# Window-attention block on one core: attention and projection on four 64x64 quadrants of the array, with a reordered round

## Chip, cores, metric

The kernel runs on one core of one Trainium2 chip. Its time is the device time of one launch in microseconds (us); the figure of a kernel is the median of its runs. Engines are called by the profile's names: PE (TensorE, matmuls), PEld (PE's weight loads), DVE (VectorE), ACT (ScalarE), POOL (GpSimd), SP (SyncE, which issues most DMAs).

## What is computed

The input is 32 images of 64 channels and 16x16 pixels, in fp32. The reference, cut to what matters:

```python
x = x + _conv_bn(x, dw0_w, dw0_s, dw0_b, groups=C)          # 3x3 depthwise
x = x + _ffn(x, f0_w1, ..., f0_b2)                          # 64 -> 128 -> 64
x = x + _windowed_attn(x, wq, wkv, pos, scale_p, dwc_w, dwc_b, proj_w, proj_b)
x = x + _conv_bn(x, dw1_w, dw1_s, dw1_b, groups=C)
x = x + _ffn(x, f1_w1, ..., f1_b2)
# _windowed_attn: windows of 7x7 of the padded 21x21 image, 4 heads of 16
q = (relu(q) + 1e-06) / sc;  k = (relu(k + pos) + 1e-06) / sc
q, k = _focus(q), _focus(k)            # t**3, scaled back to the norm of t
z = 1.0 / (einsum('bic,bc->bi', q, k.sum(axis=1)) + 1e-06)
kv2 = einsum('bjc,bjd->bcd', k, v);  y = einsum('bic,bcd,bi->bid', q, kv2, z)
y = y + depthwise_5x5(v) + dwc_b       # within the window
return y @ proj_w.T + proj_b
```

## The kernel before

The 32 images are worked in NG = 8 groups g of four images. A tile such as `x2[:, g, :]` has 128 partitions (`a` = 0 or 1 picks the partition half, 64 channels each) and 512 columns (`j` = 0 or 1, each image's 256 pixels): four images as 2 x 2. There are 16 stages `m`: m = 0 to 7 are the first depthwise convolution and FFN of group m, m = 8 to 15 the second ones of group m-8. Between them stands the attention of the group. The instruction streams of all engines are written out by hand and are held together by semaphores (`wait_ge`); each engine runs its own stream in order.

The main loop has one **round** for each n = 2 to 8. In round n, PE does in this order: `project_qkv` of group n-1 (L570, L580); `attend` of group n-3 (L645); `turn_fm` of group n-5, a transpose of the 5x5 convolution's result (L691, L695); `key_sum` of group n-2 (L613 to L615); `ffn2` of stage n+1 (L543); `key_value` of group n-2 (L601, L605); `conv` of stage n+2 (L513); `project_out` of group n-5 (L703); `turn_q` of group n-2 (L625, L628); in rounds 4 and 8 the 5x5 window convolution of four groups, `window_conv` (L665, and L671 for the bottom rows); and `ffn1` of stage n+2 (L533). In rounds 2 to 4 there is no `turn_fm` and no `project_out`.

DVE has in a round: `k_raw` (L811), `q_t` (L803), `k_t` (L819), `q_dot` (L856), `cubes` (L827), `residual` (L795), `q_sum` (L861), `add_fm` (L893), `q_scale`, `q_final` (L883, L886), `attended` (L903), `norm2` (L831), `norm6` (L835 to L837), `k_focus` (L850). ACT has: `take_v` (L375, L377), `take_y` (L413), `squares` (L384), `sixth` (L390), `take_kv` (L407), `widened` (L360), `take_qt` (L398), in rounds 4 and 8 `take_fm` (L424), `ratio` (L394), `hidden` (L368). POOL masks the values for `key_value`.

After the last round a written-out tail works off groups 4 to 7 and the stages 11 to 15. The second convolution reads its input through memory: `attended(g)` fills `x3`, a DMA writes it out (`bounce` on SP for g < 5, `write_back` on ACT for g = 5 to 7), and three DMAs of `spread(g)` read it back in a shifted form into `xr`, for which `conv(8+g)` waits.

PSUM has 8 banks of 128 x 512 fp32. Bank 0 holds the convolution, the result of `ffn2` and that of `attend`; banks 1 and 2 (`P_H`) hold the two halves of `ffn1`, and in turn `turn_fm` (1) and `project_out` (2); banks 3 to 7 hold q, k and v of a group, and later `key_value` (3 to 5) and `key_sum` (6, 7).

`attend` multiplies each of the 9 windows of an image with that window's 64x64 matrix. An image of partition half a uses rows and columns of the array at 64a, so the two halves of the array's diagonal work side by side and the other two quadrants stand idle:

```python
src = qt[p, j, :].rearrange("p (h w) -> p h w", w=HW)[:, ry, rx]
dst = ps[p, PX * j:PX * j + PX]
last = eng.matmul(dst, kv[p, slot, :], src, start=True, stop=True)
```

`project_out` is one matmul of 512 columns with a 128x128 weight matrix whose off-diagonal 64x64 blocks are zero. In fp32 each matmul of the program shows as two weight loads and two matmul records in the trace.

## Time and profile before

| | us |
|---|---|
| median of the 3 timed runs | 191.64 |
| lowest, highest | 189.98, 191.72 |
| time of the profiled execution | 189.52 |
| span of the profiled execution | 187.7 |

The span runs from the first to the last instruction of the program on the core; 1.8 us of the profiled execution's own time lie outside it. PE is busy for 93% of the span, DVE for 68%, ACT for 48%, POOL for 19%. A row of the timeline gives the start, the busy time, the engine, the line of the kernel, what is written and read, the number of records, and in brackets how long the engine had been idle before and what released it. The engines' records overlap, so the length of a step is best read as the distance between two starts.

### The profile page before, as it was taken

To read this page: it belongs to the slowest core of one execution; us is meant where nothing else is said; L and a number is where in the kernel's file an instruction comes from. 1 tells how busy PE (TensorE), PEld (TensorE's weight loads), DVE (VectorE), ACT (ScalarE), POOL (GpSimd) and SP (SyncE) were. 2 spreads that over 40 slices of the span, in tenths; PEclk is the share of its full clock that TensorE was granted. 3 is DMA by queue.
4 is the path that set the end of the run, shared out by engine and by line. 5 is a ranking of instruction groups with operands and counts; after the bars stand their busy time and mean duration, and the time that the engine had idled before them with its cause. 6 is when DMAs were issued, how large, how long until landed. Compare 5 with 4: busy or idle time off the path is not lost.

```text
span 187.7 us, 4600 instructions
## 1 busy us (share of the span) xinstructions
PE 173.9 (93%) x1874; PEld 94.7 (50%) x1874; DVE 127.5 (68%) x245; ACT 90.8 (48%) x148; POOL 36.0 (19%) x79
## 2 busy tenths in 40 slices
PE   7989868999999999899989989998998999999982
PEld 6423223537537549673674475375286652642310
DVE  3653897399899592459859886895971396148851
ACT  1474362584494595348265455734843205512340
POOL 3000180062071080006202600900620000000000
PEclk9999999999999999999999999999999999999998
DMA  5999860609600000000260170153126025994931
GB/s 144 233 260 235 159 161 2 161 3 200 191 2 3 0 0 3 3 0 0 71 170 3 59 175 3 56 155 82 59 71 166 0 80 182 268 223 128 236 105 64
DMA packets 16150, 19.33 MB, mean 103 GB/s; under 512 B 3216, under 2 KB 11664, under 8 KB 16128
## 3 DMA queue, kind: packets, MB, share of 16 engines
q1 hardware_dynamic: 15552, 17.86, 39.2%
q10 hardware_dynamic: 576, 1.17, 1.9%
q8 instruction: 15, 0.25, 0.6%
q14 instruction: 7, 0.06, 0.1%
HBM read 14.70 MB, written 4.33 MB: 101 GB/s over the span
## 4 chain that ended last, share of the span: by engine, by line
PE 66%; DVE 22%; ACT 5%; issue 4%; POOL 0%; DVEq 0%; ACTq 0%; POOLq 0%
PE ps L513 13%; PE ps L543 8%; PE ps L533 5%; PE ps L703 5%; PE ps L613 4%; PE ps L601 4%; PE ps L505 4%; PE ps L665 4%; PE ps L645 4%; DVE nrm L835 3%; DVE nrm L831 3%; PE ps L709 3%; PE ps L605 3%; DVE kraw L811 2%; DVE t L827 2%
## 5 line engine op out<-in xcount | busy, mean ns | idle before, releaser
L344 POOL TENSOR_SCALAR vmt<-vbot,cst 128x64 f32<-128x64 f32 x48 | 17.0, 377 | 100.6 <-PE ps L605 80.1
L513 PE MATMUL ps<-xr,dwst 96*32 96x480 f32 (+1 forms) x288 | 32.1, 579 | 0.0
L368 ACT ACTIVATE hid<-ps,fst 128x512 f32<-128x512 f32 x32 | 20.1, 680 | 18.2 <-PE ps L533 18.2
L407 ACT ACTIVATE kv<-ps,cst 128x288 f32<-128x288 f32 x32 | 19.8, 785 | 8.6 <-PE ps L605 8.6
L533 PE MATMUL ps<-x,w1t 64*128 64x512 f32 x64 | 18.1, 638 | 4.8 <-ACT x L360 3.1
L543 PE MATMUL ps<-hid,w2t 128*64 128x512 f32 x64 | 18.4, 618 | 1.6 <-ACT hid L368 1.6
L645 PEld LDWEIGHTS ps<-qt,kv 64*64 64x64 f32 x576 | 17.4, 135 | 2.7 <-issue 2.6
L513 PEld LDWEIGHTS ps<-xr,dwst 96*32 96x32 f32 x288 | 8.3, 109 | 20.3 <-issue 19.5
L645 PE MATMUL ps<-qt,kv 64*64 64x14 f32 (+2 forms) x576 | 18.1, 210 | 0.0
L390 ACT ACTIVATE s<-t 128x1152 f32<-128x1152 f32 x8 | 9.3, 1163 | 17.5 <-DVE t L827 15.0
L334 POOL TENSOR_SCALAR vmb<-vband,cst 128x512 f32<-128x512 f32 x24 | 17.7, 750 | 0.0
L856 DVE TENSOR_TENSOR q<-ps,t 128x576 f32<-128x576 f32 x8 | 6.1, 758 | 15.1 <-PE ps L615 15.1
L570 PEld LDWEIGHTS ps<-wqkv,x 64*128 64x128 f32 x128 | 11.1, 186 | 5.3 <-issue 5.0
L850 DVE TENSOR_TENSOR kf<-t,foc 112x512 f32<-112x512 f32 (+1 forms) x16 | 6.6, 454 | 8.9 <-ACT foc L394 8.9
L570 PE MATMUL ps<-wqkv,x 64*128 64x192 f32 x128 | 12.5, 327 | 0.0
L375 ACT ACTIVATE vband<-ps 128x512 f32<-128x512 f32 x8 | 4.8, 597 | 15.1 <-DVE tqk L803 15.1
L601 PE MATMUL ps<-vmb,kf 128*64 128x192 f32 x128 | 11.8, 327 | 0.0
L601 PEld LDWEIGHTS ps<-vmb,kf 128*64 128x64 f32 x128 | 9.1, 137 | 5.0 <-issue 4.0
L893 DVE TENSOR_TENSOR y<-y,ps 128x512 f32<-128x512 f32 x8 | 5.4, 680 | 8.9 <-ACT y L413 5.5
L533 PEld LDWEIGHTS ps<-x,w1t 64*128 64x128 f32 x64 | 5.0, 184 | 12.8 <-ACT x L360 5.4
L827 DVE TENSOR_TENSOR t<-sq,tqk 128x1152 f32<-128x1152 f32 x8 | 10.8, 1356 | 0.3 <-ACT sq L384 0.3
L613 PE MATMUL ps<-kf,cst 128*128 128x512 f32 x16 | 8.7, 624 | 2.2 <-ACT vbot L377 2.2
(113 smaller groups left out, 259.9 us busy)
## 6 DMA issues: line engine op xcount, KB each, us to landing
xr<-x_out SPq DMA_DIRECT2D x16, 264.0 KB, 4.6
xr<-in_x SPq DMA_DIRECT2D x16, 240.0 KB, 5.4
xr<-x_out SPq DMA_DIRECT2D x8, 272.0 KB, 3.6
xr<-in_x SPq DMA_DIRECT2D x8, 256.0 KB, 4.4
out<-y SPq DMA_DIRECT2D x8, 256.0 KB, 3.3
x_out<-x SPq DMA_DIRECT2D x5, 272.0 KB, 2.1
x_out<-x ACTq DMA_DIRECT2D x3, 272.0 KB, 3.2
tband<-in_matrix SPq DMA_DIRECT2D x1, 784.0 KB, 6.1
```

The source lines that it names most:

```text
L334: last = eng.tensor_scalar(vmb[:, w, :, :], vband[:, g, :, :], cc("win_band")[:, w:w + 1], 0.0, ALU.mult, ALU.add)
L344: last = eng.tensor_scalar(vmt[:, w, :], vbot[:, g, :], cc("win_bot")[:, w:w + 1], 0.0, ALU.mult, ALU.add)
L368: eng.activation(hid[:, m % 2, a, :], bank(P_H + a), ACT.Relu, bias=ff(f"f{s}b1")).then_inc(h_ready, 1)
L407: last = eng.activation(kv[:, :, :].rearrange("p (k s) c -> p k (s c)", k=3)[:, :, h:384:NH], src[:, :, h:384:NH], ACT.Copy, scale=cc("hea ...
L513: last = eng.matmul(dst[:, :, max(-dx, 0):HW - max(dx, 0)], dwst[:, s, tile % 2, dx + 1, :], taps_of(m, tile, dx), start=(dx == 0), stop=( ...
L533: eng.matmul(bank(P_H + a), w1t[p, s, :], x1[p, m % 2, :], start=True, stop=True).then_inc(h_ps, 1)
L543: last = eng.matmul(ffn_bank(m)[64 * a:64 * a + 64], w2t[:, s, :], hid[:, m % 2, a, :], start=True, stop=True)
L570: eng.matmul(qkv()[:, 4 * a + t, 0:3 * C], x2[p, g, at:at + 128], wqkv[p, :, :].rearrange("p s c -> p (s c)"), start=True, stop=True)
L601: eng.matmul(ps[64 * a:64 * a + 64, o:o + 192], kf[:, 4 * a + t, :], vmb[:, :, 2 * t + a, :], start=True, stop=True)
L613: eng.matmul(ps[:, o:o + 512], cc("mask_band"), kf[:, 0:8, :].rearrange("p s c -> p (s c)"), start=True, stop=True)
L645: last = eng.matmul(dst, kv[p, slot, :], src, start=True, stop=True)
L827: eng.tensor_tensor(t3[:, g % 2, :, :], sq[:, :, :], tqk[:, g % 2, :, :], ALU.mult).then_inc(t3_ready, 1)
```

## The change

1. **Attention on four quadrants.** In `attend` the images of j = 1 write to the other partition half: the operands stay at 64a and the output goes to 64(a^1). The loop over j is moved inside the loop over windows, and j selects the bank (0 or 1). `attend` therefore also waits until the first half of `hidden` has emptied bank 1, and `take_y` reads two banks.
2. **Projection on four quadrants.** `project_out` becomes four matmuls of 256 columns with 64x64 weights, into two banks, and turns the sides back. `turn_fm` moves to bank 2 (3 for the last group).
3. **Sides of the values.** `take_v` writes `vband` so that the convolved values of j = 1 come out on the other side; it takes two instructions in place of one. `key_value` reads its slots accordingly. The table `tbot` of the bottom rows grows from 128x16x64 to 128x16x128, with its blocks permuted, and the 32 matmuls of 64x64 become 16 of 128x128.
4. **Order.** PE: `key_sum` stands behind `ffn2`; in the tail `conv(11)` stands ahead of `key_value(7)`. DVE: `k_focus` moves from the end of a round to behind `q_t` of the next, `residual` from behind `cubes` to ahead of `q_dot`. ACT: `take_y` ahead of `take_v`, `hidden` ahead of `ratio`, and in the tail `widened(11)` ahead of `take_kv(7)`.

```diff
-        tbot = sb("tbot", 128, HD, 64)
+        tbot = sb("tbot", 128, HD, 128)
...
+        def project_at(g):
+            return 3 if g in (4, 5, 7) else 1
+
         def turn_bank(g):
-            return bank(1 if g < NG - 1 else 3)
-
-        def project_bank(g):
-            return bank(2 if g < NG - 1 else 4)
+            return bank(2 if g < NG - 1 else 3)
...
             for n in range(2, LAST):
                 g1, g2 = n - 1, n - 2
                 if n > 2:
+                    take_y(g2 - 1)
                     take_v(g1)
-                    take_y(g2 - 1)
...
+                hidden(n + AHEAD)
                 ratio(g1)
-                hidden(n + AHEAD)
...
             def key_value(g):
                 eng.wait_ge(kf_ready, g + 1)
                 eng.wait_ge(vm_ready, 2 * (g + 1))
+                if g == NG - 1:
+                    eng.wait_ge(x3_ready, 6)
...
+                eng.wait_ge(h_ready, 2 * (g + 2 * AHEAD + 1) - 1)
+                for wy in range(3):
+                    for wx in range(3):
+                        ry, rx = slice(WR * wy, min(WR * wy + WR, HW)), slice(WR * wx, min(WR * wx + WR, HW))
+                        for j in range(GP):
                             slot = (6 * j + 3 * wy + wx if wy < 2 else 12 + 3 * j + wx)
                             for a in range(2):
+                                src = qt[rows(a), j, :].rearrange("p (h w) -> p h w", w=HW)[:, ry, rx]
+                                dst = bank(P_Y + j)[rows(a ^ j), 0:PX]
                                 dst = dst.rearrange("p (h w) -> p h w", w=HW)[:, ry, rx]
-                                last = eng.matmul(dst, kv[p, slot, :], src, start=True, stop=True)
+                                last = eng.matmul(dst, kv[rows(a), slot, :], src, start=True, stop=True)
...
                     for dc in range(HD):
-                        for p in (slice(0, 64), slice(64, 128)):
-                            last = eng.matmul(out_ps[p, 16 * dc:16 * dc + 16], tbot[p, dc, :],
-                                              vbot[p, gs, NH * dc:NH * dc + NH], start=True, stop=True)
+                        last = eng.matmul(out_ps[:, 16 * dc:16 * dc + 16], tbot[:, dc, :],
+                                          vbot[:, gs, NH * dc:NH * dc + NH], start=True, stop=True)
...
-                eng.matmul(project_bank(g), ww("proj"), y[:, g, :],
-                           start=True, stop=True).then_inc(pj_ps, 1)
+                for j in range(GP):
+                    at = slice(PX * j, PX * j + PX)
+                    for side in range(2):
+                        last = eng.matmul(bank(project_at(g) + j)[rows(side ^ j), 0:PX], ww("proj")[rows(side), rows(side)],
+                                          y[rows(side), g, at], start=True, stop=True)
+                last.then_inc(pj_ps, 1)
...
+                ffn2(n + AHEAD - 1)
                 key_sum(g2)
-                ffn2(n + AHEAD - 1)
                 key_value(g2)
...
             turn_fm(6)
+            conv(11)
             key_value(7)
             project_out(6)
-            conv(11)
...
                 if n > 2:
                     k_raw(g1)
                     q_t(g1)
+                    k_focus(g2)
                     k_t(g1)
+                residual(n + AHEAD - 1)
...
                 cubes(g1)
-                residual(n + AHEAD - 1)
                 q_sum(g2)
...
-                k_focus(g1)
+            k_focus(7)
```

PE's stream in round 6, from `turn_fm` (L691) to `turn_q` (L625), before:

```order
L691 MATMUL ps<-cst,fmbot 64x2x32 x2
L695 MATMUL ps<-cst,fmband 128x112 x4
L613 MATMUL ps<-kf,cst 128x512
L614 MATMUL ps<-kf,cst 128x64
L615 MATMUL ps<-padk,cst 128x64
L543 MATMUL ps<-hid,w2t 64x512 x2
L601 MATMUL ps<-vmb,kf 64x192 x8
L605 MATMUL ps<-vmt,kf 64x384 x2
L513 MATMUL ps<-xr,dwst 32x512 x4
L513 MATMUL ps<-xr,dwst 32x32x15 x8
L703 MATMUL ps<-y,wts 128x512
L625 MATMUL ps<-cst,q 64x2x32 x2
```

The same place in the changed kernel, whose line numbers are shifted (L556 is `ffn2`, L628 to L630 `key_sum`, L720 `project_out`):

```order
L705 MATMUL ps<-cst,fmbot 64x2x32 x2
L709 MATMUL ps<-cst,fmband 128x112 x4
L556 MATMUL ps<-hid,w2t 64x512 x2
L628 MATMUL ps<-kf,cst 128x512
L629 MATMUL ps<-kf,cst 128x64
L630 MATMUL ps<-padk,cst 128x64
L616 MATMUL ps<-vmb,kf 64x192 x8
L620 MATMUL ps<-vmt,kf 64x384 x2
L526 MATMUL ps<-xr,dwst 32x512 x4
L526 MATMUL ps<-xr,dwst 32x32x15 x8
L720 MATMUL ps<-y,wts 64x256 x4
L640 MATMUL ps<-cst,q 64x2x32 x2
```

`ffn2` has moved ahead of `key_sum`, and the projection is four matmuls of 64x256.

DVE's stream at the start of round 4, from the norms of the round before, before:

```order
L836 RECIPROCAL nrm<-nrm 128x18
L837 TENSOR_TENSOR nrm<-nrm 128x18
L850 TENSOR_TENSOR kf<-t,foc 112x512
L850 TENSOR_TENSOR kf<-t,foc 128x64
L811 TENSOR_TENSOR kraw<-ps,pose 128x576
L803 SCALAR_TENSOR_TENSOR tqk<-ps,etile 128x9x64
L819 SCALAR_TENSOR_TENSOR tqk<-kraw,etile 128x9x64
L856 TENSOR_TENSOR q<-ps,t 128x576
L827 TENSOR_TENSOR t<-sq,tqk 128x1152
L795 SCALAR_TENSOR_TENSOR x<-ps,fst,x 128x512
L861 TENSOR_REDUCE den<-q 128x36
```

and in the changed kernel (L829 is `k_raw`, L868 `k_focus`, L813 `residual`, L874 `q_dot`):

```order
L854 RECIPROCAL nrm<-nrm 128x18
L855 TENSOR_TENSOR nrm<-nrm 128x18
L829 TENSOR_TENSOR kraw<-ps,pose 128x576
L821 SCALAR_TENSOR_TENSOR tqk<-ps,etile 128x9x64
L868 TENSOR_TENSOR kf<-t,foc 112x512
L868 TENSOR_TENSOR kf<-t,foc 128x64
L837 SCALAR_TENSOR_TENSOR tqk<-kraw,etile 128x9x64
L813 SCALAR_TENSOR_TENSOR x<-ps,fst,x 128x512
L874 TENSOR_TENSOR q<-ps,t 128x576
L845 TENSOR_TENSOR t<-sq,tqk 128x1152
L879 TENSOR_REDUCE den<-q 128x36
```

`k_focus` has moved behind `q_t`, and `residual` ahead of `q_dot`.

## Rows read from the trace of the kernel before

**Rows 1.** The page, part 1: busy time, share of the span, instructions.

```profile
PE 173.9 (93%) x1874; PEld 94.7 (50%) x1874; DVE 127.5 (68%) x245; ACT 90.8 (48%) x148; POOL 36.0 (19%) x79
```

**Rows 2.** The chain of waits in round 6: start, us, what.

```profile
111.56 0.60 ACT vband L375
```

**Rows 3.** The timeline of PE: one whole round, and the ends of rounds 7 and 8.

```profile
106.14 1.13 PE L533 MATMUL ps<-x,w1t 64*128 64x512 f32 x4
...
108.95 2.27 PE L645 MATMUL ps<-qt,kv 64*64 64x49 f32 x72
111.08 0.31 PE L691 MATMUL ps<-cst,fmbot 64*64 64x64 f32 x4
...
112.41 1.10 PE L613 MATMUL ps<-kf,cst 128*128 128x512 f32 x2 [0.49 <-ACT vbot L377]
...
113.97 1.08 PE L543 MATMUL ps<-hid,w2t 128*64 128x512 f32 x4
114.88 1.47 PE L601 MATMUL ps<-vmb,kf 128*64 128x192 f32 x16
...
117.07 2.68 PE L513 MATMUL ps<-xr,dwst 96*32 96x512 f32 x24
119.68 1.13 PE L703 MATMUL ps<-y,wts 128*128 128x512 f32 x2
...
121.74 1.13 PE L533 MATMUL ps<-x,w1t 64*128 64x512 f32 x4
...
137.34 3.79 PE L665 MATMUL ps<-vband,tband 112*112 112x128 f32 x32
```

**Rows 4.** The timelines of DVE and ACT in the same round.

```profile
114.08 0.76 DVE L856 TENSOR_TENSOR q<-ps,t 128x576 f32<-128x576 f32 x1 [1.95 <-PE ps L615]
...
119.72 0.63 DVE L886 TENSOR_TENSOR q<-t,den 128x64 f32<-128x64 f32 x1
```

```profile
119.81 0.69 ACT L360 ACTIVATE x<-ps,fst 128x512 f32<-128x512 f32 x1
```

**Rows 5.** The timelines of PE and DVE in rounds 2 and 3, PE in round 4.

```profile
26.77 1.65 PE L543 MATMUL ps<-hid,w2t 128*64 128x512 f32 x4 [0.86 <-ACT hid L368]
...
33.14 1.13 PE L533 MATMUL ps<-x,w1t 64*128 64x512 f32 x4 [0.81 <-ACT x L360]
34.20 1.12 PE L613 MATMUL ps<-kf,cst 128*128 128x512 f32 x2
```

```profile
35.89 0.76 DVE L856 TENSOR_TENSOR q<-ps,t 128x576 f32<-128x576 f32 x1 [3.96 <-PE ps L615]
...
49.49 0.76 DVE L856 TENSOR_TENSOR q<-ps,t 128x576 f32<-128x576 f32 x1 [0.51 <-PE ps L615]
```

```profile
69.38 3.73 PE L665 MATMUL ps<-vband,tband 112*112 112x128 f32 x32
```

**Rows 6.** Weight loads by line (count | busy, mean ns | idle), their timeline, PE's.

```profile
L543 PEld LDWEIGHTS ps<-hid,w2t 128*64 128x64 f32 x64 | 3.5, 135 | 7.9 <-ACT hid L368 5.7 <-issue 1.5
...
L589 PEld LDWEIGHTS ps<-fst,wts 128*128 128x128 f32 x2 | 0.3, 188 | 0.4 <-issue 0.4
```

```profile
82.77 0.20 PEld L543 LDWEIGHTS ps<-hid,w2t 128*64 128x64 f32 x4
```

```profile
17.02 0.30 PEld L589 LDWEIGHTS ps<-fst,wts 128*128 128x128 f32 x2 [0.44 <-issue]
```

```profile
73.03 1.94 PEld L671 LDWEIGHTS ps<-vbot,tbot 64*64 64x64 f32 x64
```

```profile
75.65 1.13 PE L533 MATMUL ps<-x,w1t 64*128 64x512 f32 x4 [0.57 <-ACT fmbot L424]
```

**Rows 7.** The tail: timelines of SP and PE, and the page's part 6 (DMA issues).

```profile
172.34 0.43 SPq L293 DMA_DIRECT2D xr<-x_out  x1
```

```profile
177.67 1.95 PE L505 MATMUL ps<-xr,dwst 96*32 96x32 f32 x32
```

```profile
xr<-x_out SPq DMA_DIRECT2D x16, 264.0 KB, 4.6
```

More of the change, by code:

```diff
@@ L241, in qkv, with rows, two_banks @@
             return ps[:, 512 * P_QKV:512 * P_QKV + 256 * NS].rearrange("p (s n) -> p s n", s=NS)
+        def rows(side):
+            return slice(64 * side, 64 * side + 64)
+        def two_banks(low):
+            return ps[:, 512 * low:512 * low + 1024].rearrange("p (k n) -> p k n", n=512)[:, :, 0:PX]
+        P_Y = 0
+        def project_at(g):
+            return 3 if g in (4, 5, 7) else 1
         def turn_bank(g):
-            return bank(1 if g < NG - 1 else 3)
-        def project_bank(g):
-            return bank(2 if g < NG - 1 else 4)
+            return bank(2 if g < NG - 1 else 3)
         def loads(m):
@@ L307, in _ @@
             for b in range(4):
-                q, o = slice(32 * b, 32 * b + 32), 32 * (b % 2)
+                q, o = slice(32 * b, 32 * b + 32), 32 * (b ^ 2 * (b % 2))
                 eng.dma_start(tbot[q, :, o:o + 32], matrix[0:32, :, 0:32]).then_inc(t_in, 16)
@@ L374, in take_v @@
                 src = qkv()[:, :, 2 * C:3 * C]
-                eng.activation(vband[:, g, :, :].rearrange("p (t a) c -> p a t c", a=2),
-                               src[:, 0:8, :].rearrange("p (a t) c -> p a t c", a=2), ACT.Copy).then_inc(v_ready, 1)
-                eng.activation(vbot[:, g, :], src[:, 8, :], ACT.Copy).then_inc(v_ready, 1)
+                dst = vband[:, g, :, :].rearrange("p (b k) c -> p b k c", k=4)
+                for a, at in ((0, slice(0, 4, 3)), (1, slice(1, 3, 1))):
+                    eng.activation(dst[:, :, at, :], src[:, 4 * a:4 * a + 4, :].rearrange("p (b j) c -> p b j c", j=GP),
+                                   ACT.Copy)
+                eng.activation(vbot[:, g, :], src[:, 8, :], ACT.Copy).then_inc(v_ready, 2)
             def squares(g):
@@ L412, in take_y @@
                 eng.wait_ge(y_ps, g + 1)
-                eng.activation(y[:, g, :], bank(0), ACT.Copy).then_inc(y_ready, 1)
+                eng.activation(y[:, g, :].rearrange("p (j n) -> p j n", j=GP), two_banks(P_Y),
+                               ACT.Copy).then_inc(y_ready, 1)
             def take_fm(c):
@@ L470, in _ @@
             write_back(5)
+            widened(LAST + AHEAD)
             take_kv(NG - 1)
             write_back(6)
-            widened(LAST + AHEAD)
             take_qt(NG - 1)
@@ L601, in key_value @@
                         eng.matmul(ps[64 * a:64 * a + 64, o:o + 192], kf[:, 4 * a + t, :],
-                                   vmb[:, :, 2 * t + a, :], start=True, stop=True)
+                                   vmb[:, :, 2 * t + (a ^ j), :], start=True, stop=True)
                 for a in range(2):
```

9 lines of the change are left out of this document (1 added, 8 removed).

## The prediction

> **What bounds the kernel now.** I read the page's busy shares first, then the chain of waits, then the timelines of the engines side by side. The shares put PE in front: busy for 173.9 of 187.7 us, against 127.5 for DVE [rows 1]. But the chain of waits does not stay on PE; in each full round it goes from DVE over ACT to PE and back. In round 6 it comes to ACT's copy of the values [rows 2], for which PE's `key_sum` waits, 0.49 us [rows 3]. So there is a loop through three engines whose length is close to PE's own work, and both have to be worked out.
>
> PE's round is the distance from one `ffn1` to the next, 106.14 to 121.74, or 15.60 us [rows 3]. Its pieces, as distances between starts: `ffn1` and q/k/v 2.81; `attend` 2.13; `turn_fm` and its wait 1.33, of which 0.49 is idle; `key_sum` 1.56; `ffn2` 0.91; `key_value` 2.19; `conv` 2.61; projection and `turn_q` 2.06. They sum to 15.60. PE has only 0.49 us of slack in it: what leaves PE can shorten the round, as long as the loop allows it.
>
> The loop, in the same round: `q_dot` starts 1.67 us behind the start of `key_sum` (112.41 to 114.08) and `widened`, the last thing `ffn1` needs, ends at 119.81 + 0.69 = 120.50, so 6.42 behind `q_dot` [rows 3, 4]. In between stand `cubes` on DVE, then `sixth` and the four copies of `take_kv` on ACT.
>
> **1. `attend`: gain 1.05 a round.** Its 36 matmuls are 72 weight loads and 72 matmul records. `attend` takes 2.13 us [rows 3]; two quadrants work side by side, so there are 36 rounds of loads, 59 ns each. The same tact stands in the bottom convolution, where only 16 columns are streamed: 64 loads in 1.94 us, two at a time, so 32 turns of 60 ns [rows 6]. It is the load of 64 columns that sets it, not the streaming. With four quadrants the 72 loads make 18 turns of 60 ns, 1.08 us, if the two column halves of one row half can load together. No row shows all four quadrants. The nearest: `ffn2` loads its two column halves twice, four loads in 0.20 us, while one load lasts 0.135 [rows 6]; so the second pair starts 0.06 behind the first, the tact of one load. I take 1.08; the other end is no gain, 2.13.
>
> The Trainium skill, "TensorE: Matmul & The Clock Gate", Part 3, has a rule against this: a load overlaps a matmul in flight only where the row group differs. The two new quadrants share their row groups with the old ones. By that rule alone `attend` would stay near 2.13. The load pairs of `ffn2`, in the same row group, speak against its strict form. It is the second rival below.
>
> **2. Projection: gain 0.46 a round.** From the projection's start to the next `ffn1` are 2.06 us [rows 3]. One matmul of 512 columns, two passes, becomes four of 256 side by side. Two passes of 512 take about 0.87 of streaming (`conv`: three turns in 2.61, rows 3), two of 256 half of it, 0.43. So 1.6 is left of 2.06. The other end is no gain.
>
> **3. The bottom table: loss 1.5, twice.** 64 loads of 64 columns, two at a time (32 turns of 60 ns), become 32 loads of 128 columns, one at a time. What such a load costs is seen where next to nothing is streamed: L589's two loads last 0.30 us together, and one of them 0.19, so the second starts 0.11 behind the first [rows 6]. 32 x 0.11 is 3.5 us in place of 2.0. PE is the path here: `ffn1` waits for ACT's `fmbot`, which waits for the last of these matmuls [rows 6]. Bounds: 1.9 (the tact of a 64-column load) and 3.6. The skill's section "LDWEIGHTS (loading the stationary operand)" on the same page says that a load costs by its columns, not its rows; the trace agrees, with 0.06 for 64 and 0.11 for 128.
>
> **4. Full rounds, 5 to 8.** Let T be the start of `ffn1`. PE's work is now 2.81 + 1.08 + 0.84 + 0.91 + 1.56 + 2.19 + 2.61 + 1.6 = 13.6. The loop: `key_sum` stands behind `ffn2`, so it starts at T + 2.81 + 1.08 + 0.84 + 0.91 = T + 5.64; `q_dot` 1.67 later; `widened` is done 6.42 later: T + 13.73. The DVE path: `q_final` ended 120.35, 6.27 behind `q_dot` [rows 4]; without `residual` (0.7, a DVE pass of the size of `q_dot`, 0.76, less its overlap) 5.6; so at T + 12.9, against `turn_q` due at T + 12.6, which puts the next `ffn1` at T + 13.8. The three lie within 0.2. I take 13.75. `take_y`, for which `ffn2` now waits (bank 0), is covered by `turn_fm`; `k_focus` has left the loop, and its new place behind `q_t` is done before `key_sum`; `take_v` now has two instructions, 0.1 more, also covered. The four rounds run from `ffn1` at 75.65 [rows 6] to the window convolution at 137.34 [rows 3], 61.7 us. Four of 13.75 are 55.0. **Gain 6.7.** Bounds: 54.4 (PE alone) and 58 (14.5 each, if the three near ties add up).
>
> **5. Rounds 2 to 4: loss 2.5.** Here the new order costs. In round 2 `key_sum` stood in the time in which `ffn2` waits for `hidden`: `ffn1` 33.14, `key_sum` 34.20, `q_dot` 35.89 [rows 5]. PE is in order, so `key_sum` now waits with it. `ffn1` ends at 34.27; the first ReLU half takes 0.7 (as ACT's L360, of the same size, rows 4), so `ffn2` starts at 35.0; where it waits like this for the second half it takes 1.65 [rows 5]; `key_sum` starts at 36.6, not 34.2: **+2.4**, and `ffn1` behind it as much later by the loop. In round 3 there is no `turn_fm` to cover `take_y`: `ffn2` waits until T + 2.81 + 1.08 + 0.14 (from the last start to the end of `attend`, 2.27 - 2.13, rows 3) + 0.65 (an ACT copy of 0.60, rows 2, and a hop) = T + 4.7, `key_sum` starts at T + 5.6 as above, and the round is 13.7 against 13.6 before; the gain of `attend` is eaten by the wait. DVE's seven instructions for the second stage's taps take 1.4 us: `q_dot` waits for `key_sum` 0.51 there, against 1.95 in another round [rows 5, 4]. They now stand between `residual`, done at T + 4.7 + 1.1 + 0.75, and `q_dot`, due at T + 7.3, a gap of 0.7: +0.7. Round 4 up to its window convolution wins 0.6, since `residual` is no longer behind `cubes`. The window convolution (69.38, rows 5) comes 2.4 + 0.1 + 0.7 - 0.6 = 2.6 later. I take 2.5; bounds 1.5 and 3.5.
>
> **6. Tail: gain 1.5.** Two `attend` (2.1) and four projections (1.8) get shorter. Against that, `attend(6)` follows `ffn1(10)` at once and must wait for a ReLU half: 0.7; `project_out(5)` waits for `add_fm(5)`, since `ffn2` between them no longer covers DVE's row of work: 0.6; `attend(7)` waits for `take_kv(7)`, `take_qt(7)` and a ReLU half, since `key_value(7)` now stands behind `conv(11)`: 0.7. That leaves 1.9. Then the DMAs. `write_back(6)` is behind `take_kv(7)` on ACT, which is not earlier than before, and SP's `spread(6)` and `spread(7)` follow it. The last `spread` issues its third DMA at 172.34, a landing takes 4.6 us, and `conv(15)` starts at 177.67 [rows 7]: 0.7 us of slack. With PE some 3 us earlier this path ends last, and gives back up to 1.5. I take 1.5 as gain; bounds 0.5 and 2.2.
>
> **Sum.** +2.5 (rounds 2 to 4) + 1.5 (bottom table) - 6.7 (rounds 5 to 8) + 1.5 (bottom table) - 1.5 (tail) = **-2.7 us**. The span goes from 187.7 to 185.0, and the profiled execution from 189.52 to 186.8. The runs shown have a median of 191.64, 2.1 above that execution; moved by the same amount they come to 188.9.
>
> **Rivals.**
> - *The ties add up.* In rounds 5 to 8 PE, the loop over ACT and DVE's row lie within 0.2 us of each other, and every semaphore hop can be missed by a little. At 14.5 a round the gain is 3.7, not 6.7, and the sum +0.3: 191.9. For it: three engines at the limit at once. Against: the rows of before already contain the hops. Chance 0.2.
> - *The quadrants take turns (slower than before).* If the column halves of one row half do not load together, `attend` stays at 2.1 and the projection at 1.06. PE's round is 15.1, four of them win 1.3; rounds 3 and 4 lose 1.05 more each, 4.6 in all; the table costs 3.0, and the tail's waits 1.4 with no gain. The sum is +7.7: 199.3. It decides at the first `attend`. For it: no row with four quadrants. Against: the load pairs of `ffn2`. Chance 0.1.
> - *The tail is not DMA-bound and the rounds run at PE's own 13.6.* Gain 7.3 and 2.2, head +2.0: -4.5, so 187.1. Chance 0.25.
> - *The forecast.* -2.7, so 188.9. Chance 0.45.
>
> **How the numbers follow.** About 1%, 1.9 us, is what a measurement of this kernel tells from no change; the three runs differ by that. Faster by over 1% are most of the forecast's case (its own range, from the bounds, is 187 to 190.5) and all of the third: 0.62. Slower by over 1% is the quadrant case and a little of the first: 0.10. The rest, 0.28, lies within 1%. The range reaches from a little past the third case to the first, 185.5 to 192, and leaves out the quadrant case.
>
> **What would show it.** In the changed profile: `attend` (L660) at 1.1 us for 72 records, and the projection (L720) 0.6; wrong if `attend` is above 1.5. The bottom matmuls (L685) 3.5 us for 32 records. `ffn1` to `ffn1` in rounds 5 to 7 between 13.6 and 14.0. The first `q_dot` at 38.3 in place of 35.89. PE idle ahead of `ffn2` in rounds 3 and 4, about 0.7, on ACT's `y`. In the tail PE waits for a DMA ahead of `conv(14)` or `conv(15)`. The forecast fails if the rounds stay above 14.5 or the first rounds lose over 4.

## The result, and the profile after

| | before | after |
|---|---|---|
| median, us | 190.82 (189.98 to 191.72) | 196.84 (195.69 to 197.53) |
| profiled execution, and its span | 189.52, 187.7 | 195.69, 193.8 |
| PE's mean granted clock, profiled execution | 0.997 | 0.964 |

The ratio after to before is 1.0296 [1.0249, 1.0344]: 3% slower, where 2.7 us (1.4%) faster was forecast. A ratio, here and below, is estimated from the runs within 1.5% of the fastest of their kernel, while the medians and ranges are of all runs, so it is not exactly the quotient of the medians. All four executions of the changed kernel have a mean granted clock between 0.947 and 0.964.

The page of after, parts 1 and 2: busy time by engine, and PE's granted clock in tenths over 40 slices.

```profile
PE 172.4 (89%) x1858; PEld 92.4 (48%) x1858; DVE 129.6 (67%) x245; ACT 89.6 (46%) x156; POOL 37.0 (19%) x79
```

```profile
PEclk9999999999999999879999999999995589999999
```

PE's busy time has hardly moved [rows 1], although `attend` and the projection halved. The clock row says where to look: two dips. The windows of after give the granted clock by stretch (us, length, busy time and records of each engine, then the clock, the DMA share and GB/s):

```profile
80.10:84.60 4.50, 4.48 (x32) 3.10 (x32) 0.00 (x0) 1.37 (x3) 0.00 (x0) 0.62 0.00 0
...
142.50:147.30 4.80, 4.12 (x36) 4.03 (x35) 0.00 (x0) 0.98 (x2) 0.00 (x0) 0.84 0.69 160
147.30:156.10 8.80, 7.97 (x91) 5.07 (x91) 1.52 (x3) 1.97 (x4) 0.00 (x0) 0.51 0.01 2
```

Both dips start at the end of a window convolution's bottom rows or right behind them. 0.51 is the lower of the two levels, 1.2 of 2.4 GHz, for nearly all of the stretch. Length times (1 - clock) gives 1.7 + 0.8 + 4.3 = 6.8 us. That is an upper estimate of the time given away: it counts the parts in which PE waits too, and a wait for ACT gets no longer at a lower clock. In the trace of before the same places are at 1.00:

```profile
75.70:78.50 2.80, 2.80 (x30) 1.86 (x30) 0.77 (x2) 1.26 (x2) 0.00 (x0) 1.00 0.03 6
...
143.80:150.00 6.20, 6.20 (x92) 4.20 (x92) 2.14 (x4) 1.86 (x3) 0.00 (x0) 1.00 0.04 8
```

The timeline of PE in after shows it from the other side:

```profile
72.27 3.73 PE L680 MATMUL ps<-vband,tband 112*112 112x128 f32 x32
75.83 3.72 PE L685 MATMUL ps<-vbot,tbot 128*128 128x16 f32 x32
80.12 1.33 PE L546 MATMUL ps<-x,w1t 64*128 64x512 f32 x4 [0.56 <-ACT fmbot L437]
...
84.56 1.23 PE L660 MATMUL ps<-qt,kv 64*64 64x49 f32 x72
...
110.20 1.13 PE L546 MATMUL ps<-x,w1t 64*128 64x512 f32 x4
...
113.02 1.23 PE L660 MATMUL ps<-qt,kv 64*64 64x49 f32 x72
114.09 0.31 PE L705 MATMUL ps<-cst,fmbot 64*64 64x64 f32 x4
...
116.07 1.12 PE L628 MATMUL ps<-kf,cst 128*128 128x512 f32 x2
...
122.50 0.66 PE L720 MATMUL ps<-y,wts 64*64 64x256 f32 x8
123.80 0.33 PE L640 MATMUL ps<-cst,q 64*64 64x64 f32 x4 [0.63 <-DVE q L904]
...
124.59 1.13 PE L546 MATMUL ps<-x,w1t 64*128 64x512 f32 x4
...
138.93 3.79 PE L680 MATMUL ps<-vband,tband 112*112 112x128 f32 x32
142.55 4.06 PE L685 MATMUL ps<-vbot,tbot 128*128 128x16 f32 x32
147.28 2.08 PE L546 MATMUL ps<-x,w1t 64*128 64x512 f32 x4 [0.68 <-ACT fmbot L437]
150.19 2.10 PE L660 MATMUL ps<-qt,kv 64*64 64x49 f32 x72 [0.83 <-ACT hid L378]
...
156.09 0.66 PE L720 MATMUL ps<-y,wts 64*64 64x256 f32 x8
...
179.80 1.95 PE L518 MATMUL ps<-xr,dwst 96*32 96x32 f32 x32 [1.28 <-DMA xr<-x_out]
```

The same four records of `ffn1` (L546) last 1.13 us in a round and 2.08 behind the second window convolution; `attend` (L660) lasts 1.23 and 2.10. When an instruction's own duration doubles, it's not a wait, and the waits view shows nothing of it.

The same instructions at full clock price the loss by rows. `ffn1` to `attend` takes 4.44 us behind the first window convolution (80.12 to 84.56) and 2.82 in a round (110.20 to 113.02): 1.6. The second bottom table takes 4.06, the first 3.72: 0.3. In the tail the run e5 below has the same order at full clock, and from `ffn1(10)` to the first projection it takes 5.41, against 8.81 here (147.28 to 156.09): 3.4. The sum is **5.3 us**. The rows of e5:

```profile
143.23 1.13 PE L546 MATMUL ps<-x,w1t 64*128 64x512 f32 x4 [0.88 <-ACT fmband L437]
...
148.64 0.66 PE L722 MATMUL ps<-y,wts 64*64 64x256 f32 x8
```

The spans differ by 6.1 us. By stretches, between the same instructions (the starts of before are in [rows 3, 5, 6]; its `ffn1` behind the second window convolution starts at 143.78):

| stretch | before | after | difference | forecast | clock, by rows |
|---|---|---|---|---|---|
| start to the 1st window convolution | 69.38 | 72.27 | +2.9 | +2.5 | |
| 1st window convolution to `ffn1` | 6.27 | 7.85 | +1.6 | +1.5 | |
| four rounds, to the 2nd window convolution | 61.69 | 58.81 | -2.9 | -6.7 | 1.6 |
| 2nd window convolution to `ffn1` | 6.44 | 8.35 | +1.9 | +1.5 | 0.3 |
| tail | 43.9 | 46.5 | +2.6 | -1.5 | 3.4 |
| sum | | | +6.1 | -2.7 | 5.3 |

Taking 5.3 from 6.1 leaves +0.8: by this estimate the change would not have been faster at full clock either. Another estimate agrees: the one run of e1 below at full clock has a span of 185.6, and two wide tables at 1.6 each bring that to 188.8, 1.1 above before and 5.0 below after. So up to 5.3 of the 8.8 us that the forecast missed by are clock. It can be less, down to some 3.4: at full clock the tail waits longer for its DMAs, 2.8 and 3.2 us in e5 and e8 against 1.3 in after, so that the fall stands in part where PE would have waited. The rest is 2.2 in the four rounds, 0.4 in the head, 0.2 at the two tables, and the tail's DMAs.

### The profile page after: what moved, and what is told of

Its sections match the earlier page's. It is cut to its first block, busy times and chain, and to the rows that moved or that the text cites. A ratio compares the mean times of both kernels' runs of the same rounds, so it can differ in the third digit from the quotient of the medians.

```text
span 193.8 us, 4584 instructions
## 1 busy us (share of the span) xinstructions
PE 172.4 (89%) x1858; PEld 92.4 (48%) x1858; DVE 129.6 (67%) x245; ACT 89.6 (46%) x156; POOL 37.0 (19%) x79
## 3 DMA queue, kind: packets, MB, share of 16 engines
q1 hardware_dynamic: 15552, 17.86, 38.3%
## 4 chain that ended last, share of the span: by engine, by line
PE 59%; DVE 15%; issue 10%; DMA 6%; ACT 6%; SPq 0%; POOL 0%; DVEq 0%; ACTq 0%; POOLq 0%
PE ps L556 7%; PE ps L546 7%; PE ps L526 7%; PE ps L583 6%; PE ps L660 5%; PE ps L685 4%; PE ps L680 4%; PE ps L628 4%; DMA x_out<-x 3%; DMA xr<-x_out 3%; PE ps L727 3%; DVE q L901 2%; PE ps L593 2%; PE ps L518 2%; ACT kv L419 2%
## 5 line engine op out<-in xcount | busy, mean ns | idle before, releaser
L546 PE MATMUL ps<-x,w1t 64*128 64x512 f32 x64 | 19.2, 676 | 5.1 <-ACT x L370 3.6
L556 PE MATMUL ps<-hid,w2t 128*64 128x512 f32 x64 | 19.0, 615 | 4.6 <-ACT hid L378 2.5
L829 DVE TENSOR_TENSOR kraw<-ps,pose 128x576 f32<-128x576 f32 x8 | 6.1, 757 | 13.1 <-PE ps L593 12.8
L583 PEld LDWEIGHTS ps<-wqkv,x 64*128 64x128 f32 x128 | 11.8, 202 | 5.8 <-issue 5.8
L370 ACT ACTIVATE x<-ps,fst 128x512 f32<-128x512 f32 x12 | 8.0, 667 | 12.9 <-PE ps L526 12.9
L583 PE MATMUL ps<-wqkv,x 64*128 64x192 f32 x128 | 13.8, 352 | 0.0
L813 DVE SCALAR_TENSOR_TENSOR x<-ps,fst,x 128x512 f32<-128x512 f32 x8 | 6.0, 751 | 10.5 <-PE ps L556 10.5
L868 DVE TENSOR_TENSOR kf<-t,foc 112x512 f32<-112x512 f32 (+1 forms) x16 | 6.5, 451 | 9.0 <-ACT foc L406 9.0
L660 PEld LDWEIGHTS ps<-qt,kv 64*64 64x64 f32 x576 | 10.1, 145 | 4.7 <-issue 4.7
L660 PE MATMUL ps<-qt,kv 64*64 64x14 f32 (+2 forms) x576 | 10.7, 219 | 1.1 <-ACT hid L378 1.1
L546 PEld LDWEIGHTS ps<-x,w1t 64*128 64x128 f32 x64 | 5.1, 192 | 12.8 <-ACT x L370 5.4
L853 DVE TENSOR_REDUCE nrm<-s 128x18 f32<-128x1152 f32 x8 | 10.7, 1339 | 0.0
L849 DVE TENSOR_REDUCE nrm<-sq 128x18 f32<-128x1152 f32 x8 | 10.7, 1338 | 0.0
```

Source lines behind the costliest of these rows:

```text
L546: eng.matmul(bank(P_H + a), w1t[p, s, :], x1[p, m % 2, :], start=True, stop=True).then_inc(h_ps, 1)
L556: last = eng.matmul(ffn_bank(m)[64 * a:64 * a + 64], w2t[:, s, :], hid[:, m % 2, a, :], start=True, stop=True)
L583: eng.matmul(qkv()[:, 4 * a + t, 0:3 * C], x2[p, g, at:at + 128], wqkv[p, :, :].rearrange("p s c -> p (s c)"), start=True, stop=True)
L660: last = eng.matmul(dst, kv[rows(a), slot, :], src, start=True, stop=True)
L849: step.mark(eng.tensor_reduce(nrm[:, 0, :], sq[:, :, :].rearrange("p s (k c) -> p (s k) c", c=C), AX_X, ALU.add))
```

## The experiments

What is open: which part of the change brings the clock down, whether work for PE in the right place holds it, and what sets the rounds and the tail. An "unused matmul" is one of 256 columns into a part of PSUM that nobody reads. Where nothing else is said, a kernel is compared with runs of before on the same chip: medians 189.94 for e1 to e4, 190.29 for e5 to e8, 191.27 for f1 to f4, 191.17 for g1 and g2.

**e2_before_wide: the kernel before, with only the wide bottom table.**

```diff
-        tbot = sb("tbot", 128, HD, 64)
+        tbot = sb("tbot", 128, HD, 128)
...
-                        for p in (slice(0, 64), slice(64, 128)):
-                            last = eng.matmul(out_ps[p, 16 * dc:16 * dc + 16], tbot[p, dc, :],
-                                              vbot[p, gs, NH * dc:NH * dc + NH], start=True, stop=True)
+                        last = eng.matmul(out_ps[:, 16 * dc:16 * dc + 16], tbot[:, dc, :],
+                                          vbot[:, gs, NH * dc:NH * dc + NH], start=True, stop=True)
```

> The kernel before with its bottom table at 128 columns (block diagonal, 16 matmuls of 128x128 in place of 32 of 64x64) and nothing else. Theory (clock): 3.3 us for the loads and a fall of the granted clock behind one or both window convolutions, in all 195.5 to 200 against 190.8. Rival (waits): 3.3 us alone, 194.1, granted clock 1.00 throughout.

201.74 us, ratio 1.0581 [1.0519, 1.0643]. The profiled run is the slowest of the four, 203.72. Its windows, and PE's timeline at the first table and behind the second:

```profile
69.00:76.50 7.50, 7.50 (x68) 7.44 (x67) 2.45 (x4) 3.39 (x6) 1.42 (x3) 1.00 0.01 2
76.50:83.30 6.80, 6.24 (x45) 4.20 (x45) 1.49 (x3) 1.76 (x4) 0.00 (x0) 0.50 0.00 0
...
148.00:165.30 17.30, 16.62 (x114) 10.40 (x113) 4.46 (x7) 2.36 (x5) 0.00 (x0) 0.51 0.05 11
```

```profile
72.84 3.72 PE L670 MATMUL ps<-vbot,tbot 128*128 128x16 f32 x32
...
150.44 2.08 PE L533 MATMUL ps<-x,w1t 64*128 64x512 f32 x4 [0.68 <-ACT fmbot L424]
```

In the median this kernel is 11.8 us above before. Some 3.2 of it is what the matmuls themselves take longer, so 8.6 are left for the clock; length times (1 - clock) of the profiled run, 6.8 x 0.50 + 17.3 x 0.49 = 11.9, is the upper estimate for that run. The wide table alone, in a kernel with none of the other parts, brings the clock down twice and makes it worse than the whole change. Ahead of the fall PE is not idle by the records: it loads 128 columns of weights and streams 16, over and over, for 3.7 us, and then waits 0.6 to 0.7 for `fmbot`, as before did behind its 64-column version without a fall.

**g1_wide_64 and g2_wide_128: e2, where each of the table's 16 matmuls (32 records) streams 64 or 128 columns in place of 16.** The loads and the waits stay. The columns come from a constant table in place of the values, so these two kernels leave out the bottom rows.

```diff
-                        last = eng.matmul(out_ps[:, 16 * dc:16 * dc + 16], tbot[:, dc, :],
-                                          vbot[:, gs, NH * dc:NH * dc + NH], start=True, stop=True)
+                        last = eng.matmul(out_ps[:, 16 * dc:16 * dc + 64], tbot[:, dc, :],
+                                          wts[:, 0:64], start=True, stop=True)
```

> The kernel before with the wide bottom table, as e2, but each of its 32 matmuls streams 64 columns of a constant table in place of the 16 of the values (the bottom rows of the 5x5 convolution are therefore not computed). By the records of e2 one matmul takes 0.11 us whatever it streams up to here, so the table should still take 3.7 us. Theory (what brings the clock down in e2 is how little is streamed between the loads): the clock stays at 1.00 behind both window convolutions, or falls for less than in e2; about 193 to 195 us. Rival (it is the 128-column loads, or the stretch as a whole, whatever is streamed): clock 0.5 behind both as in e2, 200 to 203 us.

> As g1, with 128 streamed columns in each matmul (the bottom rows are not computed either). The table takes 3.7 to 4 us. Theory: no fall behind either window convolution, clock 0.99 to 1.00, 193 to 194.5 us. If 64 columns were not enough but 128 are, g1 is near e2 and this one at 194. Rival (the loads): as e2, 200 to 203 us.

194.09 us, ratio 1.0166 [1.0076, 1.0255], and 194.31, 1.0148 [1.0066, 1.0231]; clock 1.00 in seven of the eight runs, 0.991 in one. The same windows and rows as above, of g1:

```profile
69.00:76.50 7.50, 7.50 (x71) 7.41 (x69) 2.70 (x4) 3.64 (x6) 1.67 (x3) 1.00 0.01 2
76.50:83.30 6.80, 6.24 (x113) 5.07 (x112) 2.92 (x5) 3.16 (x8) 0.00 (x0) 1.00 0.01 2
```

```profile
73.10 3.76 PE L670 MATMUL ps<-wts,tbot 128*128 128x64 f32 x32
...
147.18 1.13 PE L533 MATMUL ps<-x,w1t 64*128 64x512 f32 x4 [0.68 <-ACT fmbot L424]
```

The stretch lasts as long as in e2 (3.76 and 3.72 us), PE is as busy by its records, the waits behind it are the same (0.56 and 0.68), and the clock holds. So the 128-column loads alone do not bring it down, and the 3 us by which g1 is slower than before are the loads' own price. What differs from e2 is the number of streamed columns, and also what is streamed: constants in place of values. Not tried is the control, 16 columns of the same constants; that it's the number is the likelier reading, not a shown one. The load hides the streaming of 64 columns and, but for 0.06 us, that of 128 (3.82 in g2).

**e1_bot64: the changed kernel with the table 64 wide again.** The sides are then turned in `turn_fm`, whose two small matmuls become three (`pick` is the identity in blocks of 32 columns).

```diff
-        tbot = sb("tbot", 128, HD, 128)
+        tbot = sb("tbot", 128, HD, 64)
...
-                    eng.matmul(v[p, :, PX - 32:PX], fmbot[p, g, :], ident[p, p], start=True, stop=True)
+                eng.matmul(v[rows(0), :, PX - 32:PX], fmbot[:, g, :], pick[:, 0:4:3, :], start=True, stop=True)
+                for j in range(GP):
+                    eng.matmul(v[rows(1), j, PX - 32:PX], fmbot[:, g, :], pick[:, 2 - j, :], start=True, stop=True)
```

> The changed kernel with the bottom table back at 64 columns and 32 matmuls of 64x64; the sides of j = 1 are swapped in turn_fm instead. Theory (clock): the 16 matmuls with 128x128 weights and 16 columns cost 1.7 us each time they run, and the granted clock falls behind them (0.62 over 4.5 us, 0.84 over 4.8 us, 0.51 over 8.8 us in the changed kernel, together 6.8 us of lost clock). Without them the clock stays at 1.00 and the time falls by 8 to 10 us, from 196.8 to 187 to 189. Rival (waits): the clock falls because attend(6) now waits for hidden and PE idles there; then only the loads come back, 3.3 us, 193.5, and the clock still falls behind round 8.

The four runs lie at 187.43, 192.66, 195.33 and 197.86, with a clock of 1.00, 0.961, 0.965 and 0.946: so far apart that no ratio stands. The windows of the second, and PE's row behind round 8:

```profile
70.00:82.00 12.00, 11.41 (x204) 9.06 (x199) 4.91 (x11) 7.20 (x14) 3.26 (x6) 1.00 0.01 3
...
141.00:155.60 14.60, 13.08 (x128) 7.49 (x130) 4.37 (x7) 2.35 (x5) 0.00 (x0) 0.53 0.08 18
```

```profile
141.97 2.08 PE L546 MATMUL ps<-x,w1t 64*128 64x512 f32 x4 [0.69 <-ACT fmbot L437]
```

In this run the dip behind round 4 is gone, the one behind round 8 has stayed, 6.9 us by length times (1 - clock) and 5.1 by rows (13.51 us from `ffn1(10)` to the second projection, 8.37 in e5). So the table isn't the whole cause. `ffn1(10)` is already at 2.08 us: this fall starts ahead of the wait of `attend(6)`, behind a narrow table and a wait of 0.69 that before has as well. The single run at full clock, 187.43 with a span of 185.6, is what the change is worth without the wide table and the loss of clock.

**e6_attend_wait: the kernel before, where `attend(6)` also waits for the first half of `hidden(10)`,** as the change makes it do.

```diff
                 eng.wait_ge(x1_ready, g + 2 * AHEAD + 1)
+                if g == 6:
+                    eng.wait_ge(h_ready, 21)
```

> The kernel before with one more wait: attend(6) waits for the first half of hidden(10), as in the changed kernel, 0.75 us of idle PE. Rival (this wait brings the clock down behind round 8): the clock falls in most runs, 193 to 197. Theory (it does not, since the fall starts ahead of ffn1): full clock, at most 0.8 us more, 190.0 to 190.8.

194.88 us, ratio 1.0218 [1.0131, 1.0304], clock 0.974 to 0.982 in all four runs. PE's timeline and the window:

```profile
144.48 1.13 PE L533 MATMUL ps<-x,w1t 64*128 64x512 f32 x4 [0.69 <-ACT fmbot L424]
146.44 3.44 PE L647 MATMUL ps<-qt,kv 64*64 64x49 f32 x72 [0.83 <-ACT hid L368]
```

```profile
146.40:158.00 11.60, 11.56 (x100) 7.68 (x100) 3.64 (x5) 1.07 (x2) 0.00 (x0) 0.56 0.00 0
```

Here my theory, that this wait doesn't bring the clock down, was wrong. A wait of 0.83 us, with nothing else changed, costs 4.6 us in the median. In the profiled run 4.5 are the clock by rows (146.44 to 158.22 from `attend(6)` to the third projection behind it, in before 144.84 to 152.10), and `attend` takes 3.44 in place of 2.27. The engine had run the 16-column matmuls, waited 0.69, worked for 1.1, and waited again.

**f1_wait_filled: e6, and three unused matmuls ahead of `attend(6)`.** The wait stays; PE has work in it.

```diff
+            for k in range(3):
+                eng.matmul(ps[:, 512 * 7 + 256:512 * 8], ident, wts[:, 0:256], start=True, stop=True)
             attend(6)
```

> e6_attend_wait (the kernel before with the one added wait of attend(6), 194.9 and a clock of 0.97 to 0.98 in all runs) with three matmuls into unused PSUM columns placed ahead of attend(6), which fill the time in which PE waited. They compute nothing that is used. Theory (idle PE next to the quiet stretch brings the clock down): full clock in nearly all runs, 190.5 to 191.3. Rival (another property of the wait): no change, 194 to 196.

191.66 us over 10 runs, ratio 1.0072 [1.0030, 1.0114]; clock 1.00 in six of them, 0.991 in three, 0.974 in one.

```profile
146.42 1.56 PE L750 MATMUL ps<-wts,cst 128*128 128x256 f32 x6
147.91 2.27 PE L647 MATMUL ps<-qt,kv 64*64 64x49 f32 x72
```

```profile
76.30:80.00 3.70, 3.70 (x26) 2.53 (x23) 0.11 (x1) 1.26 (x2) 0.00 (x0) 0.54 0.02 4
...
145.00:158.00 13.00, 12.61 (x132) 7.86 (x134) 6.99 (x15) 2.07 (x5) 0.00 (x0) 1.00 0.12 32
```

The matmuls take 1.49 us ahead of `attend(6)`, the kernel is 0.7% slower than before by the ratio, where e6 was 2.2%, and in the profile the fall behind round 8 is gone. So for the kernel before the effect of this wait is shown from both sides. One run of the ten, at 0.974, fell further and wasn't profiled. What remains in the profile is a short dip behind round 4, at a place where this kernel is the kernel before, instruction for instruction. Before itself stands near the edge: its 13 runs on this chip have clocks of 0.978 to 0.999, and the four slowest, 191.94 to 192.69, are all at 0.991 or below.

**e8_filler: e1, and three unused matmuls behind round 8's window convolution, ahead of `ffn1`.**

> e1_bot64 with three matmuls of 128x128 weights and 256 columns into unused PSUM columns behind round 8's window convolution: they do nothing but fill the 0.7 us in which PE waits for fmbot. Theory (quiet stretch): the clock stays at 1.00 in all or nearly all runs, 187.5. Rival: the rounds of before it bring the clock down, no change against e1_bot64.

189.68 us, ratio 0.9872 [0.9780, 0.9963], clock 0.982 to 1.00, where e1 had 0.946 to 1.00. In its profile the stretch from 140 to 160 us is at 1.00, though `attend(6)` still waits 0.86. In this run it was enough to fill the first of the two waits. A dip behind round 4, which was not filled, gives away up to 1.7.

**e5_bot_mid: e1, with the bottom rows as the third of the window convolution's five parts,** so that matmuls of 128 columns follow them.

```diff
-        FM_PARTS = [2, 0, 1, 3, 4, 0, 2, 3, 1, 4]
+        FM_PARTS = [2, 0, 4, 3, 1, 0, 2, 4, 1, 3]
```

> e1_bot64 with the bottom rows' part of the window convolution third instead of last, between two parts with 128-column matmuls. In e1_bot64 one run of four kept the full clock (187.43) and three did not (192.7 to 197.9); in the profiled one the clock fell 0.3 us ahead of ffn1(10), behind the bottom matmuls and the wait for fmbot. Theory (quiet stretch): 2 us of small matmuls and 0.7 us of waiting stand side by side there; apart, the clock stays at 1.00 in all runs, 187.5. Rival (less PE work in every round, or the wait of attend(6)): still two or three runs of four near 192 to 197.

190.74 us over 10 runs, ratio 0.9983 [0.9930, 1.0036], clock 0.97 to 1.00 and no dip in the profile. The clock is better held than in e1, but 1.00 in all runs, as expected, was missed: three of the ten are at 0.998 or above, seven at 0.97 to 0.99. And the span of the profiled run, 187.9, is no shorter than before's though its clock is 0.999: PE waits 0.56 and 2.20 us for the DMAs of the last two convolutions. The clock alone doesn't make the change pay.

**e3_sum_first: the changed kernel, `key_sum` ahead of `ffn2` in round 2 alone,** and `residual` back behind `cubes` there.

```diff
+                if n == 2:
+                    key_sum(g2)
                 ffn2(n + AHEAD - 1)
-                key_sum(g2)
+                if n > 2:
+                    key_sum(g2)
```

> The changed kernel with key_sum ahead of ffn2 in round 2 alone (DVE: residual behind cubes there). Theory (round 2 is paid on the path): q_dot of round 2 comes 2.4 us earlier, and the time falls by 1.7 to 2.4 us, 194.5 to 195.1. Rival: the later rounds or the DMAs of the tail absorb it, no change, 196.8.

194.37 us, ratio 1.0200 [1.0144, 1.0256]. The first window convolution starts at 70.57, in place of 72.27: 1.7 us of the 2.9 that the head lost. The clock still falls twice.

**e4_j_outer: the changed kernel, with the loop over j outside the windows again in `attend`.** Each matmul still has its own quadrant, but neighbours in the stream take turns on two only.

> The changed kernel with attend's loop over j outside again: the same 36 matmuls into the same quadrants, but only two quadrants are in use at a time. Prices the four quadrants. Theory (PE sets the rounds): attend goes from 1.07 back to 2.1 us, eight times, and the rounds 5 to 8 from 14.3 to 15.1; in all 5 to 8 us more, 202 to 205. Rival (the loop over DVE and ACT sets the rounds): at most 2 us more, below 199.

205.47 us, ratio 1.0792 [1.0733, 1.0851]. PE's timeline of one `attend`, which starts at 116.90 and ends at 118.96:

```profile
116.90 1.90 PE L660 MATMUL ps<-qt,kv 64*64 64x49 f32 x66
...
118.76 0.20 PE L660 MATMUL ps<-qt,kv 64*64 64x4 f32 x2
```

2.06 us from the first start to the last end, against 1.23 for the same 72 records in the other order (2.27 in before). Four quadrants help only if the four stand next to each other in the instruction stream. The profiled run is the slowest of the four, 209.07; behind round 8 it has 18.0 us at 0.53, twice as long as in after.

**e7_tail: e1 and e3 together, and in the tail `key_sum(7)` ahead of `attend(6)`,** with `ratio(7)` ahead of `hidden(10)` and one store of the output moved behind the reads of `spread(4)`.

```diff
+            eng.wait_ge(qt_ready, 7)
+            key_sum(7)
             attend(6)
             turn_fm(4)
-            key_sum(7)
```

> e1_bot64 with key_sum ahead of ffn2 in round 2; key_sum(7) ahead of attend(6) in the tail, with ratio(7) ahead of hidden(10), so that PE works while it waited for hidden; and store(2) behind spread(4) on SP, so that bounce(4) is issued 1.3 us earlier. Theory: at full clock 187.4 less 2.4 (round 2) less 0.5 to 1.5 (tail), 183.5 to 184.7; if PE's wait at attend(6) takes part in the fall of the clock, all runs are there, otherwise some are 5 to 10 us longer. Rival (the DMAs of the tail set the end): 186 at full clock.

187.81 us, ratio 0.9834 [0.9748, 0.9919]; clock 0.954, 0.981, 0.991, 0.989. Expected were 183.5 to 184.7 at full clock, which no run reached. `key_sum(7)` is work that PE has anyway and now stands in the wait. That isn't enough in every run; the windows of the profiled one (192.9):

```profile
57.00:61.00 4.00, 4.00 (x22) 2.80 (x20) 2.15 (x4) 1.97 (x4) 0.00 (x0) 0.57 0.00 0
...
142.00:157.00 15.00, 14.22 (x136) 8.00 (x137) 6.01 (x13) 1.86 (x3) 0.00 (x0) 0.54 0.18 51
```

Here the clock fell behind round 8 with the second wait filled, and the first, 0.69 for `fmbot`, left; e8 filled the first and left the second, and held. And the fall at 57 us stands far from any window convolution, behind a wait of 1.28 for `q_final`. After has that wait too (1.26) and no fall there.

**f3_filled: e7, and three unused matmuls behind both window convolutions.**

> e7_tail (bottom table at 64 columns, key_sum first in round 2, key_sum(7) ahead of attend(6), store(2) later) with the unused matmuls behind both window convolutions. Theory: the clock stays up in all runs, and the median falls from 187.8 to 185.3 to 186.5, with less spread. Rival (the DMAs of the tail set the end and the clock only moves the waits for them): 187, PE waiting longer ahead of conv(15).

187.71 us (187.04 to 188.26), ratio 0.9809 [0.9743, 0.9875], clock 0.996 to 0.998 in all four runs. PE's timeline, two rounds and the last convolution:

```profile
91.79 1.13 PE L551 MATMUL ps<-x,w1t 64*128 64x512 f32 x4
...
105.87 1.13 PE L551 MATMUL ps<-x,w1t 64*128 64x512 f32 x4
...
120.27 1.13 PE L551 MATMUL ps<-x,w1t 64*128 64x512 f32 x4
...
176.00 1.94 PE L523 MATMUL ps<-xr,dwst 96*32 96x32 f32 x32 [2.00 <-DMA xr<-x_out]
```

This version is 1.9% faster than before, and no run has a long fall. By the ratio it is no faster than e7, only steadier. Expected were 185.3 to 186.5; what came is the rival's 187, with PE waiting 2.00 us for the DMA ahead of the last convolution.

**f2_after_filled: the changed kernel as it is, with unused matmuls behind both window convolutions and ahead of `attend(6)`.**

> The changed kernel, wide bottom table and all, with the same unused matmuls behind both window convolutions and ahead of attend(6). Prices the clock in the changed kernel itself. Theory: the clock comes back for the most part, and with it up to 6.8 us: 190 to 193, where what is left over the kernel before is the wide table's 3.3 us. Rival (the wide table's matmuls alone, 3.5 us of them, bring the clock down whatever stands behind them, as in e2_before_wide): one fall per window convolution is left, 193 to 196.

194.83 us, ratio 1.0171 [1.0080, 1.0262], clock 0.973 to 0.991; the 190 to 193 that I expected were missed. In the profiled run, the slowest (197.08), the fall behind round 8 is gone, but behind round 4 it comes already within the wide table's own matmuls:

```profile
76.21 4.66 PE L685 MATMUL ps<-vbot,tbot 128*128 128x16 f32 x32
80.70 2.91 PE L766 MATMUL ps<-wts,cst 128*128 128x256 f32 x6
```

Unused matmuls behind the table come too late for that. Behind the same table in round 8 the clock held in the same run, so they help at times. It held more surely without the wide table (f3) or with more columns streamed (g1).

**f4_fm_early: f3, with `add_fm` ahead of `q_dot` in DVE's stream.**

```diff
                     residual(n + AHEAD - 1)
+                if 0 <= c:
+                    add_fm(c)
...
-                if 0 <= c:
-                    add_fm(c)
```

> f3_filled with DVE's add_fm in the gap between residual and q_dot. In the changed kernel the rounds 5 to 8 took 14.1 to 14.4 us, not 13.75, with PE waiting 0.3 to 0.6 for q_final ahead of turn_q. Theory (DVE's path to q_final sets the rounds): it gets 0.6 shorter, the rounds 13.7, and x3 is out earlier, so 1.5 to 2.4 us less than f3_filled. Rival (the loop over ACT or the tail's DMAs set it): under 0.5 us less.

187.58 us, ratio 0.9829 [0.9751, 0.9906]: the same as f3, where 1.5 to 2.4 less was expected. PE's row of the last convolution and a window of the tail:

```profile
173.81 2.55 PE L523 MATMUL ps<-xr,dwst 96*32 96x32 f32 x32 [1.93 <-DMA xr<-x_out]
```

```profile
174.00:179.00 5.00, 5.00 (x40) 1.15 (x30) 1.38 (x2) 0.00 (x0) 0.00 (x0) 0.66 0.17 59
```

The rounds take 13.93 (`ffn1` at 91.01 and 104.94), against 14.08 and 14.40 in f3: so DVE's row up to `q_final` set them, and not PE or the loop over ACT. Of the 0.6 taken out of that row only 0.15 to 0.47 came back, since PE now waits 0.33 for `attended`, further down DVE's stream. The tail starts 2.1 us earlier (`ffn1` behind round 8 at 139.99, in f3 at 142.09), and the last convolution starts 2.2 earlier too (173.81 against 176.00). But behind the DMA wait the clock falls, 5.0 x 0.34 = 1.7 us, and the span is only 0.5 shorter (185.5 against 186.0).

## Why the prediction was wrong

The step that failed is one that wasn't there: every duration of the sum was taken at the full clock, because the trace of before shows it nearly everywhere. None of the rivals had a clock in it. The runs showed a loss of clock of up to 5.3 us in its place. Two terms were mis-sized besides: the four rounds won 4.5 at full clock and not 6.7, and the DMAs of the tail took more than the sum gave them. Point by point:

- **1, `attend`: right.** 1.07 us from its start to `turn_fm` (113.02 to 114.09), forecast 1.08. The Trainium skill, "TensorE: Matmul & The Clock Gate", Part 3, lets a load overlap a matmul in flight only where the row group differs; the trace doesn't agree: both orders take turns on the two row groups alike, and the same matmuls take 1.23 us in one and 2.06 in the other (e4).
- **2, projection: right.** From its start to the next `ffn1` 2.09 (122.50 to 124.59), of which 0.63 is a wait: 1.46, forecast 1.6.
- **3, bottom table: the duration right, the consequence missed.** L685 takes 3.72 (3.5), and the stretch grows by 1.6 (1.5). What it does to the clock is worth more than its 3.2 us: 8.6 in e2. By its records PE is busy all through them; with 64 or 128 columns streamed there (g1, g2) the clock held.
- **4, rounds: mis-sized.** 14.07, 14.39 and 14.34 behind the first, forecast 13.75; with the 16.01 of the first, of which 1.6 are clock, the four lost 2.2 of the forecast gain besides the clock. `key_sum` starts at T + 5.87, not 5.64 (110.20 to 116.07): `ffn2` and the transposes take 0.1 more each than the rows of before gave. `q_dot` follows 1.69 later (1.67), but `q_final` ends 5.98 behind it, not 5.6: of the 0.7 of `residual` taken out of that row only 0.3 was won. The row is 0.67 shorter up to `q_final`, whose first two instructions then take 1.14 in place of 0.76 (in three of the four rounds; the second has 0.76 and is the one of 14.07). The three engines lie close, as I said, and DVE was the last of them. The first rival ("the ties add up", 14.5) was nearer than the forecast. The rows are, of after's DVE:

```profile
122.05 1.14 DVE L901 TENSOR_TENSOR q<-t,den 128x256 f32<-128x256 f32 x2
123.11 0.63 DVE L904 TENSOR_TENSOR q<-t,den 128x64 f32<-128x64 f32 x1
```

- **5, rounds 2 to 4: right.** +2.9, forecast +2.5. `q_dot` of round 2 starts at 38.62 (38.3), and PE waits for ACT's `y` in round 3, 0.81 (0.7). e3 wins back 1.7 of it.
- **6, tail: PE's terms right, the DMAs mis-sized, one consequence missed.** Less its DMA wait (1.28) and the clock (3.4), the tail of after is 41.8 us. Less their DMA waits, those of e5 and e8 at full clock are 41.9 too (44.7 - 2.8 and 45.1 - 3.2). That is 2.0 less than the 43.9 of before, and the terms ahead of the DMAs came to 1.9. But I let the DMAs take back only 0.4, of up to 1.5. At full clock they took back 2.8 and 3.2, and those tails are 0.8 and 1.2 us longer than before's. The wait that `attend(6)` was said to gain, 0.7, is 0.83. It was priced as 0.7 us; e6 shows that in the kernel before it costs 4.6.

The conditions that I wrote down ("the forecast fails if the rounds stay above 14.5 or the first rounds lose over 4") would hardly have caught it: the first rounds lost 2.9, and only the round with the first dip, at 16.01, is above 14.5. The narrower sign, 13.6 to 14.0 in rounds 5 to 7, failed in all three (16.01, 14.07, 14.39). They asked for waits, and the larger loss isn't in a wait.

Shown by runs: that the wide table alone brings the clock down (e2), that more columns of a constant in its place do not (g1, g2), that in the kernel before the wait ahead of `attend(6)` alone does (e6), and that work put in that wait takes the fall away (f1). For the changed kernel itself the second cause isn't shown: behind round 8 the clock is down before that wait begins in after (0.84 from 142.5 on) and in e1, and it falls in e7, where that wait is filled. Filling the wait for `fmbot` held it in e8's profile. Why the changed kernel falls there behind a narrow table, as before seldom does, stays open; that less work of PE in each round prepares it wasn't tried. Not tried either: the changed kernel with wider streams at its bottom table. Open are also why before's own clock holds in most executions and not in all, and why `q_final` takes 0.4 longer in most rounds.
